# First attention of an audio tower: scores laid 192 apart, two groups turned in three blocks, one exponential pass per four groups

## The reference, cut to what matters

```
q, k, v = x @ Wq.T + bq, x @ Wk.T + bk, x @ Wv.T + bv          # 12 heads of 16 numbers
score[h,t,s] = sum_d ws[d] * tanh(q[h,t,d] + k[h,s,d]) + bs     # 179 x 179 for each head
p_attn = softmax(score, axis=-1)
attn = p_attn @ v;   out = attn @ Wo.T + bo
```

## Time and profile before

| | |
|---|---|
| profiled execution | 1448.74 us, span 1446.8 us |
| runs | 1444.05 to 1456.63 us, median 1449.03 |
| PE busy | 1153.0 us (80%) |
| DVE busy | 1105.7 us (76%) |
| ACT busy | 1003.6 us (69%) |
| POOL busy | 861.9 us (60%) |
| mean granted TensorE clock | 0.943 |
| tanh, L917 | 688.8 us busy in 272 passes |
| exponential, L906 | 95.3 us busy in 144 passes |

### The profile page before, as it was taken

How to read it: one execution, slowest core, us unless ns; L and a number is a source line. 1 busy time by engine, 2 the same in 40 slices (tenths; PEclk the granted TensorE clock), 3 DMA queues, 4 the chain that set the end, 5 groups by cost and what they waited for, 6 DMA issues and landing times. The chain is left out here.

```text
span 1446.8 us, 39002 instructions
## 1 busy us (share of the span) xinstructions
PE 1153.0 (80%) x16164; PEld 874.5 (60%) x16164; DVE 1105.7 (76%) x2109; ACT 1003.6 (69%) x921; POOL 861.9 (60%) x978
## 2 busy tenths in 40 slices
PE   4766898788778887887788779847999999989496
PEld 3544665566556655665566458835667666767396
DVE  8797998899889998998899867753566677665443
ACT  1389999999999999999999967732234433433142
POOL 4098878887888788888888977540012222123354
PEclk9899999999999999999999999975899999988698
DMA  9999997000000000000000002000000100010352
GB/s 254 360 360 356 352 344 246 2 2 2 2 2 2 2 2 2 2 3 2 1 2 2 2 15 53 0 1 1 2 2 12 59 17 15 12 39 9 94 152 65
DMA packets 75449, 103.06 MB, mean 71 GB/s; under 512 B 6303, under 2 KB 73640, under 8 KB 75282
## 3 DMA queue, kind: packets, MB, share of 16 engines
q1 hardware_dynamic: 63784, 87.90, 18.5%
q10 hardware_dynamic: 6860, 6.12, 1.6%
q0 software_dynamic: 4640, 6.65, 1.4%
HBM read 18.32 MB, written 83.85 MB: 71 GB/s over the span
## 5 line engine op out<-in xcount | busy, mean ns | idle before, releaser
L917 ACT ACTIVATE work<-work 128x2864 f32<-128x2864 f32 (+1 forms) x272 | 688.8, 2578 | 32.2 <-DVE work L436 31.3
L436 POOL TENSOR_TENSOR work<-shared 128x1253 f32<-128x1253 f32 (+1 forms) x272 | 613.5, 2267 | 151.6 <-PE psum L1789 117.8
L1789 PE MATMUL psum<-work,ws_place 128*32 128x179 f32 x8640 | 397.6, 325 | 165.8 <-ACT work L917 165.6
L436 DVE TENSOR_TENSOR work<-psum,shared 128x1611 f32<-128x1611 f32 (+3 forms) x288 | 486.5, 1722 | 0.6
L1789 PEld LDWEIGHTS psum<-work,ws_place 128*32 128x32 f32 x8640 | 261.7, 112 | 274.4 <-ACT work L917 214.2
L1979 PE MATMUL psum<-shared 32*64 32x179 f32 (+1 forms) x1728 | 142.5, 367 | 8.1 <-DVE shared L1497 8.1
L756 POOL TENSOR_TENSOR tsum<-tstats 128x4 f32<-128x4 f32 (+1 forms) x16 | 3.7, 233 | 200.8 <-DVE tstats L1414 200.8
L1276 DVE SCALAR_TENSOR_TENSOR p_sb<-psum,bs_col,s_top 128x358 f32<-128x358 f32 x144 | 82.1, 570 | 43.9 <-PE psum L1802 30.7
L1979 PEld LDWEIGHTS psum<-shared 32*64 32x64 f32 (+1 forms) x1728 | 81.1, 159 | 56.5 <-issue 36.5
L1503 DVE TENSOR_SCALAR pt_region<-pt_region 128x1074 uint32<-128x1074 uint32 x48 | 34.6, 721 | 98.4 <-ACT pt_region L988 98.4
L906 ACT ACTIVATE pt_region<-psum,bs_neg 128x512 f32<-128x512 f32 x144 | 95.3, 663 | 1.6 <-PE psum L1802 1.5
(11 more groups left out here) (365 smaller groups left out, 1984.2 us busy)
## 6 DMA issues: line engine op xcount, KB each, us to landing
xs_dram<-pad_row SPq DMA_DIRECT2D x23, 3088.0 KB, 27.6
pt_region<-xs_dram ACTq DMA_DIRECT2D x19, 193.0 KB, 2.6
pt_region<-xs_dram SPq DMA_DIRECT2D x19, 193.0 KB, 2.4
xs_dram<-pad_row SPq DMA_DIRECT2D x1, 2895.0 KB, 27.0
work<-in_x SPq DMA_DIRECT2D x2, 768.0 KB, 10.1
work<-in_x ACTq DMA_DIRECT2D x2, 768.0 KB, 16.2
work<-in_L_ffn_W2T SPq DMA_DIRECT2D x1, 1536.0 KB
work<-in_L_ffn_W1T SPq DMA_DIRECT2D x1, 1536.0 KB
```

Source lines behind the costliest of these rows:

```text
L436: ins = eng.tensor_tensor(dst[:, a * KEEP:e * KEEP].rearrange("p (u s) -> p u s", s=KEEP), k[:, h * KP:h * KP + KEEP].unsqueeze(1).to_broa ...
L917: act.activation(a, a, ACT.Tanh).then_inc(tanh_done, 1)
L1789: ins = pe.matmul(bank_s[p % 2][32 * quad:32 * quad + 32, at:at + KEEP], ws_place[:, j, :], arg_slot(n)[:, u * KEEP:(u + 1) * KEEP], start ...
```

## The change

Scores are written to `p_sb` 192 columns apart (`ROW`). A duo is then 371 columns and is turned as three blocks of 128: keys 0 to 127 of the even group; keys 128 to 178 of the even group with keys 0 to 63 of the odd one; keys 64 to 178 of the odd group. `pt` has three blocks by nine duos. ACT takes two duos, four groups, in one pass out of both turning banks, 768 columns, four times a batch, and the last group in a pass of 256: five passes. The passes stand after the tanhs 8, 12 and 16 of the batch and 2 and 4 of the next. The turn of duo 8 moves from group 2 to group 3.

The odd groups' keys now lie on other partitions than V does, so V is arranged twice more (`v_extra`) by three DMAs a batch that SP issues. The 24 filling DMAs are issued between them, two behind each of the first twelve batches' three. `context` runs over even and odd groups apart: 32 products of 96 columns and 32 of 48 in place of 16 of 180 and 16 of 92 or 88, each product f32 and recorded as two instructions, as before. Small edits go with it: POOL clears `v_extra` and one more piece of `stage`, DVE adds `bs` to all of `p_sb` at the start (384 columns in place of 77, twice), and three semaphores are shared.

```diff
+EXPS = -(-DUOS // 2)
+ROW, HALF_K, LAST_K = 192, 64, KEEP - 64
...
-        pt = [... 2 * (n + 1) * PT_COLS].rearrange("p (s c) -> p s c", s=2) for n in range(2)]
+        pt = [... 3 * DUOS * 128].rearrange("p (s k c) -> p s k c", s=3, k=DUOS) for n in range(2)]
+        v_extra = [... 2 * HEADS * VC].rearrange("p (s h v) -> p s h v", s=2, h=HEADS) for n in range(2)]
...
+            for b in range(B):
+                n, v = b % 2, v_sb[b % 2]
+                sp.wait_ge(v_ready, b + 1)
+                need(sp, v_spread[n], 48 * (b // 2))
+                sp.dma_start(v_extra[n][HALF_K:128, 0, :, :], v[0:HALF_K, 0, :, :]).then_inc(v_spread[n], 16)
+                sp.dma_start(v_extra[n][0:HALF_K, 1, :, :], v[HALF_K:128, 0, :, :]).then_inc(v_spread[n], 16)
+                sp.dma_start(v_extra[n][HALF_K:LAST_K, 1, :, :], v[0:TB, 1, :, :]).then_inc(v_spread[n], 16)
+                for k in range(2 * b, min(2 * b + 2, FILLS)):
+                    fill(k)
...
-            def exps(b, k):
-                p, w = b * DUOS + k, duo(k)
-                if k == 0:
+            def exps(b, q):
+                if q == 0:
                     need(act, ctx_psum, 2 * b - 2)
-                act.wait_ge(turned, p + 1)
-                act.activation(pt[b % 2][:, :, 256 * k:256 * k + 128 * w],
-                               bank_pt[p % 2].rearrange("p (s c) -> p s c", s=2)[:, :, 0:128 * w],
-                               ACT.Exp, bias=bs_neg[:, :], scale=1.0).then_inc(exp_done, 1)
+                act.wait_ge(turned, b * DUOS + min(2 * q + 2, DUOS))
+                if q < EXPS - 1:
+                    banks = psum[:, 4 * 512:6 * 512].rearrange("p (k c) -> p k c", k=2)[:, :, 0:384]...
+                    ins = act.activation(pt[b % 2][:, :, 2 * q:2 * q + 2, :]..., banks, ACT.Exp, ...)
+                else:
+                    ins = act.activation(pt[b % 2][:, 0:2, 2 * q, :], bank_pta[:, 0:256]..., ACT.Exp, ...)
+                ins.then_inc(exp_done, 1)
...
-                    if g % 2 and g >= 7 and real(b):
-                        exps(b, (g - 7) // 2)
-                    if g in (0, 2, 3, 4) and real(b - 1):
-                        exps(b - 1, DUOS - 4 + (0, 2, 3, 4).index(g))
+                    if g in (8, 12, 16) and real(b):
+                        exps(b, (g - 8) // 4)
+                    if g in (2, 4) and real(b - 1):
+                        exps(b - 1, 2 + g // 2)
...
             def turn_duo(b, k):
-                bank, src = bank_pt[p % 2], p_sb[p % 2]
+                bank, src = bank_pt[k % 2], p_sb[p % 2]
                 pe.wait_ge(smax_done, p + 1)
-                need(pe, exp_done, p - 1)
-                for a in range(duo(k)):
-                    for s in range(2):
-                        ins = pe.transpose(bank[:, 256 * s + 128 * a:256 * s + 128 * a + 128],
-                                           src[:, a * KEEP + 128 * s:a * KEEP + 128 * s + 128], ident[:, :])
+                need(pe, exp_done, b * EXPS + k // 2)
+                for s in range(duo(k) + 1):
+                    ins = pe.transpose(bank[:, 128 * s:128 * s + 128], src[:, 128 * s:128 * s + 128], ident[:, :])
                 ins.then_inc(turned, 1)
...
-            def context(b, r, col):
+            def context(b, r):
+                n = b % 2
+                keys = [pt[n][:, s, :, :].rearrange("p k (i c) -> p k i c", c=32) for s in range(3)]
+                parts = [[(v_sb[n][:, 0, :, :], keys[0]), (v_sb[n][:, 1, :, :], keys[1])],
+                         [(v_extra[n][:, 0, :, :], keys[1]), (v_extra[n][:, 1, :, :], keys[2])]]
                 if r < 2:
-                    spans = [(0, UA // 4, 16 * r, col)]
+                    spans = [(KP * r, 16 * r, ((0, 6, 0), (0, 6, 16)))]
                 else:
-                    spans = [(UA // 4, PT_COLS // 32, 16 * n, col + UB * n) for n in range(2)]
+                    spans = [(100 * m, 16 * m, ((6, 9, 16), (5, 8, 0))) for m in range(2)]
+                for at, c, groups in spans:
+                    for odd, (lo, hi, shift) in enumerate(groups):
                         for j in range(4):
...
-                    if g in (0, 1, 2):
-                        turn_duo(c, DUOS - 3 + g)
+                    if g in (0, 1, 3):
+                        turn_duo(c, (DUOS - 3, DUOS - 2, 0, DUOS - 1)[g])
                     if g == 5:
-                        pe.wait_ge(exp_done, DUOS * b)
+                        pe.wait_ge(exp_done, EXPS * b)
                         pe.wait_ge(v_ready, b)
+                        pe.wait_ge(v_spread[c % 2], 48 * (c // 2 + 1))
```

More of the change, by code:

```diff
@@ L79, in build @@
         pt_region = sb("pt_region", [128, 9216])
-        pt = [pt_region[:, 2 * n * PT_COLS:2 * (n + 1) * PT_COLS].rearrange("p (s c) -> p s c", s=2) for n in range(2)]
+        pt = [pt_region[:, 2 * n * PT_COLS:2 * n * PT_COLS + 3 * DUOS * 128].rearrange("p (s k c) -> p s k c", s=3, k=DUOS) for n in range(2)]
+        v_extra = [pt_region[:, 2 * n * PT_COLS + 3 * DUOS * 128:2 * n * PT_COLS + 3 * DUOS * 128 + 2 * HEADS * VC].rearrange(
+            "p (s h v) -> p s h v", s=2, h=HEADS) for n in range(2)]
         shared = sb("shared", [128, 4352])
@@ L130, in build @@
         bs_neg = sb("bs_neg", [128, 1])
-        p_sb = [sb(f"p_sb{n}", [128, KEEP + WIDE]) for n in range(2)]
+        p_sb = [sb(f"p_sb{n}", [128, 2 * ROW]) for n in range(2)]
         inv_sum = sb("inv_sum", [128, 2, HEADS])
@@ L302, in build @@
         v_ready = sem("v_ready")
+        v_spread = [sem(f"v_spread{n}") for n in range(2)]
         args_dve = sem("args_dve")
@@ L504, in _, with fill @@
             sp.wait_ge(pad_ready, 2)
[L505 to L508, removed]
+            def fill(n):
+                lo = 2048 * n
+                rows = min(2048, XS_ROWS - lo) // 128
+                sp.dma_start(xs_dram[lo:lo + 128 * rows, :].rearrange("(j p) d -> p j d", p=128),
+                             pad_row[:, :].unsqueeze(1).to_broadcast([128, rows, RW])).then_inc(e_zeroed, 16)
+            FILLS = -(-XS_ROWS // 2048)
+            for b in range(B):
[7 more added lines that the diff above has]
+                    fill(k)
             def load_expert(dst, loaded, r, wt, bias):
@@ L574, in _ @@
             pool.memset(mx3[:, :], 0.0).then_inc(w1_step, 1)
+            for n in range(2):
+                pool.memset(v_extra[n][:, :, :, :], 0.0)
             pool.memset(pad_row[:, :], 0.0).then_inc(pad_ready, 1)
@@ L724, in _ @@
             pool.wait_ge(wq_step, 6)
-            pool.memset(stage[2][:, 1, 0:D], 0.0)
+            for n in (2, 3):
+                pool.memset(stage[n][:, 1, 0:D], 0.0)
             pool.memset(ew2[:, 1, :], 0.0).then_inc(ew_blank, 1)
@@ L898, in _ @@
             act.preload_act_table_set("exp_and_others")
[L900 to L903 removed]
+            def exps(b, q):
+                if q == 0:
                     need(act, ctx_psum, 2 * b - 2)
[L905 to L908 removed]
+                act.wait_ge(turned, b * DUOS + min(2 * q + 2, DUOS))
+                if q < EXPS - 1:
+                    banks = psum[:, 4 * 512:6 * 512].rearrange("p (k c) -> p k c", k=2)[:, :, 0:384].rearrange("p k (s c) -> p k s c", s=3)
+                    ins = act.activation(pt[b % 2][:, :, 2 * q:2 * q + 2, :].rearrange("p s k c -> p k s c"), banks,
+                                         ACT.Exp, bias=bs_neg[:, :], scale=1.0)
+                else:
+                    ins = act.activation(pt[b % 2][:, 0:2, 2 * q, :], bank_pta[:, 0:256].rearrange("p (s c) -> p s c", s=2),
+                                         ACT.Exp, bias=bs_neg[:, :], scale=1.0)
+                ins.then_inc(exp_done, 1)
             for b in range(B + 1):
@@ L1107, in small_consts @@
                 for n in range(2):
-                    dve.tensor_scalar(p_sb[n][:, 2 * KEEP:KEEP + WIDE], p_sb[n][:, 2 * KEEP:KEEP + WIDE], bs_col[:, :], None, ALU.add)
+                    dve.tensor_scalar(p_sb[n][:, :], p_sb[n][:, :], bs_col[:, :], None, ALU.add)
                 for j in range(4):
@@ L1275, in smax @@
                 dve.wait_ge(top_step, p + 1)
-                dve.scalar_tensor_tensor(p_sb[p % 2][:, 0:w * KEEP].rearrange("p (a s) -> p a s", s=KEEP), s, bs_col[:, :],
+                dve.scalar_tensor_tensor(p_sb[p % 2][:, 0:w * ROW].rearrange("p (a s) -> p a s", s=ROW)[:, :, 0:KEEP], s, bs_col[:, :],
                                          top.unsqueeze(2).to_broadcast([128, w, KEEP]),
@@ L1558, in gate_move @@
                 ins.then_inc(gate_out, 1)
-            rsteps = [0]
+            rsteps = [wlink[0]]
             def rlink(ins):
@@ L1815, in context @@
                         for j in range(4):
-                            ins = pe.matmul(bank_out[32 * j:32 * j + 32, at:at + 4 * (hi - lo)].rearrange("p (i c) -> p i c", c=4),
-                                            v_sb[b % 2][:, s, 4 * r + j, :], tile[:, lo:hi, c + 4 * j:c + 4 * j + 4],
-                                            start=(s == 0), stop=(s == 1))
```

(5 more changed lines are left out.)

24 lines of the change are left out of this document (10 added, 14 removed).

## The result

The changed kernel takes 1499.68 us, median of four executions (1494.44 to 1502.74), against 1450.69 us of the kernel before on the same chip (1444.05 to 1456.63). The ratio is 1.0341, 95% interval 1.029 to 1.0391: slower by 3.4%, some 49 us. The prediction said 1466 us and a range up to 1479. Its direction holds, its size does not.

A forecast was written before the change was run, and what follows sets the result against it. ACT was taken to bound the attention. Waits of 38.6 us plus 1.9 at the ends, less 22.7 saved, gave net +17.8 on 1448.74 us: 1466 us, range 1453 to 1479.

The forecast's parts named there:

- What bounds the kernel: First attention: ACT sets the pace, 46.8 us of work plus one 1.37 us wait in a 48.18 us batch.
- what ACT saves: Exponential passes: 768 columns taken at 0.785 us, saving 1.42 us a batch, 22.7 us in 16 (bounds 13 to 33).
- The rival with a cheap pass of 0.63 us: Same waits but smaller, from a cheap wide pass or cheaper context and turns: 1452 to 1462 us; chance 0.30.
- The waits on duos 1, 3 and 5: ACT waits for PE's late turns before the passes after tanhs 8, 12 and 16: 1.5, 0.1 and 0.65 us.
- the forecast of 49.4: Attention batch: grows from 48.2 to 49.4 us.
- The floor under small matmuls: Context round 2: rival that narrower products get no cheaper, 1.5 us and not 0.91, total 1475 us; chance 0.12.
- The cover of V's copies: V's DMAs in SP's queue: wanted about 70 us after V is ready, at most two fills ahead, so no cost.
- Duo 7 and duo 8 are in time: scores 1.36 and turn 0.6 make under 2.48: Passes after tanhs 2 and 4: PE scores and turns within one tanh of 2.48 us, so ACT does not wait.
- ACT's wait at group 2 (0.44 more): ACT before tanh 2, waiting for DVE's sums: 1.81 us in place of 1.37, fifteen times.
- the chain through the turn of duo 6: Tanh 0, scores 0, turn of duo 6, `smax`, sums 2: as long as before, 4.42 us, less 0.13.
- plus some for TensorE's clock: High end of the range, 1479 us: allowance for stretches at 1.2 GHz, from a batch at 0.97 taking 48.99 us.

The follow-up runs named there:

- turn-first run: Changed kernel with the turns of duos 1 and 3 issued ahead of the former batch's context round 2 and turn back; 1490.22 us, one execution.
- the second set of small products: Changed kernel with 28, 6, 32, 28 and 16 unused products of 64 columns before PE's waits in groups 0 to 4; 1479.54 us, ratio 1.0117.
- the layout with a pass for each duo: Changed kernel with one 384-column exponential pass a duo at the old places and duo 8 turned at group 2 again; 1443.82 us, ratio 0.9901.

## Why the prediction was wrong

*What bounds the kernel, and what ACT saves: right.* The pass is 0.80 us on average where 0.785 was taken, 21.8 us saved in all for 22.7. The rival with a cheap pass of 0.63 us falls.

*The waits on duos 1, 3 and 5: right.* 1.50, none and 0.67 us for 1.5, 0.1 and 0.65. The turn-first run confirms the order behind the first. The full-clock batch of 49.46 us and the batches of the run with the second set of small products, 49.46 and 49.47, are the forecast of 49.4.

*The floor under small matmuls: no such floor here, as the prediction held likely.* Context round 2 runs from 405.03 to the turn at 405.92, 64 matmul instructions of 48 columns in 0.89 us (0.91 forecast):

```profile
405.03 0.36 PE L1845 MATMUL psum<-pt_region,v_sb 128*32 128x48 f32 x14
...
405.92 0.55 PE L1826 MATMUL psum<-ident,p_sb 128*128 128x128 f32 x3
```

That is 14 ns from start to start. The Trainium skill (TensorE: Matmul & The Clock Gate, "Wait — 56ns, not 53.3ns?") has it never below about 25 ns; for products that go around four column groups the measurement is below, and the measurement decides.

*The cover of V's copies: right.* No wait for them in after, and 98 us where the order of the queue was changed.

*"Duo 7 and duo 8 are in time: scores 1.36 and turn 0.6 make under 2.48": the step that failed.* It is true at 2.4 GHz. The prediction itself had lengthened ACT's wait at group 2 (0.44 more), and with it PE's idle there, which was 1.81 us before; it did not ask what clock PE would have after it, nor that group 3 was already scored at the low clock in some batches of before. At 1.2 GHz scores and turn are 2.55 + 0.69 us, over 2.48, and the answer is no. The same low clock lengthens the chain through the turn of duo 6, which the prediction took as long as before. The range had "plus some for TensorE's clock" at its high end, taken from a single batch at 0.97, as if the change left the clock alone. The runs put the missing term at 24 us in the attention (41.7 - 17.8). From start to start, 13.0 us of it are the 14 waits before L930, for which the sum had nothing, and 10.0 are at group 2, where 15 waits make 37.2 us for 15 x 1.81 = 27.2. The last 0.9 is the pass of 0.80 us for 0.785.

*What stays open.* The 6.9 us of the next stage. It took 100.9 us before and 107.8 after. The code there is the same in all kernels, and its time goes with its granted clock: 100.9 to 101.3 us in three executions at 1.00, 102.8 to 103.5 in eight at 0.97, 104.5 or 104.6 in three at 0.95. The changed kernel was at 0.95 too, so some 3.6 of the 6.9 us go with the clock; the other 3 are open, and no run says what makes the clock fall there. The share of the clock in the medians, 1.0341 - 1.0117 = 2.2% or 32 us, is more than the traces show: with the second set of small products the attention ends 20.5 us earlier and the next stage takes 4.7 less, 25 us together. The two ratios come from different chips, and their intervals leave some 9 us of play.

## What to carry to other kernels

Where an edit makes one engine wait at a point where PE idles too, add up PE's idle stretches there and ask what its next work costs at half the clock, above all if somebody waits for that work with less than its own length to spare. Merging passes saves a fixed cost only if the last input of the merged pass is ready when the first one was wanted; count the deadline from the latest piece. And before a wide pass is paid for, look at the buffer whose release sets the standing wait: on the layout with a pass for each duo, a third score buffer brought the ratio from 0.990 to 0.977, where the wide passes brought it to 1.034.

## What the runs showed of the hardware

- The granted clock fell to 0.50 within a PE that was busy 40.6 of 51.0 us, behind two idle stretches of 2.1 and 2.4 us, and was at 1.00 again within 8 us. The average of the batch, 0.91, does not say where it fell, and the place decides the price: four batches of the kernel before, at 0.93 to 0.96, took no longer than those at 1.00.
- An exponential over two PSUM banks, 768 columns, is 0.80 us from start to start; 384 in one bank 0.47, 512 in one bank 0.57. Two passes of 384 would be 0.94, so most of the fixed part is paid once, also over two banks.
- 32 useless products of 64 columns in bf16 took 1.10 us of idle PE time. Sets of them before groups 0 to 4 brought the changed kernel from 1.034 to 1.012 of before, and the kernel before nothing.
